# A 32-expert feed-forward sublayer: four slot tiles a step instead of two, products on column and row groups

## What is computed

```python
E = 32
H = int(D * 0.25)          # D = 128
logits = x_flat @ router_w.T + router_b
routed_idx = jnp.argmax(logits, axis=-1)
def expert_mlp(w1, b1, w2, b2):
    h = jax.nn.relu(x_flat @ w1 + b1)
    return jax.nn.relu(h @ w2 + b2)
y_all = jax.vmap(expert_mlp)(weights1, bias1, weights2, bias2)
out_flat = y_all[routed_idx, jnp.arange(n)]
...
x = _layernorm(x + _L1_ffn_ref(x, ...), axis=-1)
```

## Time and profile before

| what | value |
|---|---|
| time, median of 3 runs | 4104.81 us (4103.65 to 4107.08) |
| time of the profiled execution | 4081.88 us |
| its span | 4080.1 us |
| last load before its routing, first load of the next sublayer | 1759.8 and 2154.9 us |
| its first and last `evict` | 1859.0 and 2087.6 us |

### The profile page before, as it was taken

The page is one execution under the profiler, slowest core; times in us unless marked ns, Lnnn a source line. Parts: engine busy times, 40 slices in busy tenths (PEclk is TensorE's granted clock), DMA queues, the critical chain, the costliest instruction groups (busy, mean ns, idle before and its releaser), DMA issues. The chain is left out here.

```text
span 4080.1 us, 81328 instructions
## 1 busy us (share of the span) xinstructions
PE 3018.0 (74%) x27802; PEld 2047.6 (50%) x27802; DVE 2256.7 (55%) x6213; ACT 1718.3 (42%) x3334; POOL 1789.2 (44%) x1575
## 2 busy tenths in 40 slices
PE   3399907767777599946747996886899867997693
PEld 2387805554455356634524664554344434666572
DVE  2002336536777577751235775886777576775123
ACT  0144404334444366602214664664555554662341
POOL 2544272225565455523344554664022354552534
PEclk9999959888998799955558998998898788997896
DMA  6377611020010112114521112221000001221573
GB/s 215 115 227 218 191 41 45 6 7 24 32 41 31 53 55 73 55 41 122 136 76 41 55 53 67 76 86 59 1 1 1 1 3 47 77 67 56 160 224 106
DMA packets 305037, 304.44 MB, mean 75 GB/s; under 512 B 91108, under 2 KB 226821, under 8 KB 304648
## 3 DMA queue, kind: packets, MB, share of 16 engines
q1 hardware_dynamic: 269160, 252.01, 20.1%
q0 software_dynamic: 16384, 33.59, 2.8%
q10 hardware_dynamic: 19232, 15.50, 1.2%
HBM read 161.27 MB, written 55.84 MB: 53 GB/s over the span
## 5 line engine op out<-in xcount | busy, mean ns | idle before, releaser
L802 DVE TENSOR_TENSOR moe_first_tile_y<-moe_first_out_ps,moe_first_expert_w 128x256 f32<-128x256 f32 x78 | 33.1, 425 | 336.5 <-PE moe_first_out_ps L937 336.4
L998 POOL DMA_INDIRECT slot_x<-x_tok,moe_first_slots x128 | 123.7, 967 | 177.8 <-DVE moe_first_slots L775 75.1
L978 ACT ACTIVATE moe_first_hid<-moe_first_hid_ps,moe_first_expert_w 128x256 f32<-128x256 f32 x312 | 128.2, 471 | 155.6 <-PE moe_first_hid_ps L926 155.6
L1012 POOL DMA_INDIRECT moe_first_token_y<-slot_y,moe_first_slots x128 | 123.8, 967 | 100.4 <-issue 65.2
L1665 POOL TENSOR_TENSOR causal_k_blocks<-causal_k_T,headmask 128x1024 f32<-128x1024 f32 x64 | 121.2, 1896 | 105.9 <-PE causal_scores L1277 101.9
L2783 PE MATMUL L_ffn_experts<-L_ffn_expert_w,x_T 128*128 128x512 f32 x256 | 166.2, 735 | 1.8 <-ACT L_ffn_expert_out L2880 1.8
L1665 POOL TENSOR_TENSOR alibi_k_blocks<-alibi_k_T,headmask 128x1024 f32<-128x1024 f32 x64 | 121.2, 1896 | 105.2 <-PE alibi_scores L1277 101.2
L1665 POOL TENSOR_TENSOR full_k_blocks<-full_k_T,headmask 128x1024 f32<-128x1024 f32 x64 | 121.2, 1896 | 93.8 <-PE full_scores L1277 89.5
L937 PE MATMUL moe_first_out_ps<-moe_first_expert_w,moe_first_hid 128*128 128x128 f32 x1248 | 162.2, 281 | 0.0
L1416 ACT ACTIVATE diff_probs_T<-diff_pT 128x512 f32<-128x512 f32 x128 | 76.4, 597 | 183.0 <-PE diff_pT L1291 183.0
L1665 POOL TENSOR_TENSOR keys_k_blocks<-keys_k_T,headmask 128x1024 f32<-128x1024 f32 x64 | 120.7, 1896 | 74.7 <-PE keys_scores L1277 71.1
(11 more groups left out here) (544 smaller groups left out, 9152.3 us busy)
## 6 DMA issues: line engine op xcount, KB each, us to landing
moe_first_expert_w<-in_L_attn_experts SPq DMA_DIRECT2D x78, 578.0 KB, 4.0
moe_last_expert_w<-in_L_ffn_experts SPq DMA_DIRECT2D x46, 578.0 KB, 4.1
slot_x<-blank ACTq DMA_DIRECT2D x2, 4992.0 KB, 44.2
moe_first_tile_x<-slot_x SPq DMA_DIRECT2D x78, 128.0 KB, 4.1
slot_y<-moe_first_tile_y SPq DMA_DIRECT2D x78, 128.0 KB, 1.9
L_ffn_tile_x<-slot_x SPq DMA_DIRECT2D x64, 128.0 KB, 2.3
slot_y<-L_ffn_tile_y SPq DMA_DIRECT2D x64, 128.0 KB, 1.8
moe_last_tile_x<-slot_x SPq DMA_DIRECT2D x46, 128.0 KB, 3.9
```

Of the source, the lines that this page charges most:

```text
L802: dve.tensor_tensor(y_out[:, q, :, :], out_bank[q][:, 0:SLOT_TILE].rearrange("p (s d) -> p s d", s=SPAN), over(wall[:, j % RING, 2 * FF + ...
L978: act.activation(hid[:, j % 2, b, :], hid_bank[b // 2][:, SLOT_TILE * (b % 2):SLOT_TILE * (b % 2) + SLOT_TILE], gelu, bias=wall[:, j % RIN ...
L998: pool.indirect_dma_start(slot_x[part][:, :], bass.IndirectOffsetOnAxis(slots[:, part, r, t:t + 1], 0), net.x_tok[:, part * K + t, :], Non ...
L1012: pool.indirect_dma_start(y_in[:, p, k, r, :], None, slot_y[part][0:NT * SLOT_TILE, :], bass.IndirectOffsetOnAxis(slots[:, part, r, t:t + ...
```

## The change

Four slot tiles, a "quad" (`QUAD` = 512 rows), are one step; there are 16 steps a part, 32 in all. The four first products write to the four partition groups of one bank, [32g, 32g + 32), so that each has a 32-column group of the array; one relu of 128x128 covers all four. The second products read the hidden rows at partitions [32g, 32g + 32), so that each has a 32-row group, and each writes a bank of its own. Their bias is no longer a 33rd row but a product of its own, of 32 rows of ones with the bias row of the expert's block (its other 31 rows are zero). An expert's weights come in two transfers, `up` (128 rows of 128 B) and `down` (32 rows of 1028 B), where one of 128 rows of 644 B was. The output has one set of four banks that does not alternate. `x_in` has three places of a quad.

```diff
-    J = NT // 2
+    J = NT // 4
-    RING, XRING = 8, 4
+    RING, XRING = 4, 3
...
-        x_in = sb("tile_x", [128, XRING, 2, D])
-        hid = sb("hid", [H + 1, 2, PAIR])
+        x_in = sb("tile_x", [128, XRING, 4, D])
+        hid = sb("hid", [128, 2, TILE])
...
+        out_banks = ctx.enter_context(nc.psum_tensor(f"{name}_out_ps", [128, 4, 512], F32))
...
-        after_pair = {J + 2 + c * ((J - 4) // PC): c for c in range(PC)}
+        after_quad = {J + 2 + (5 * c + 2) // 3: c for c in range(PC)}
...
# evict
-                    dve.tensor_copy(y_out[:, q, :, :], out_bank[q][:, 0:PAIR].rearrange("p (s d) -> p s d", s=2))\
-                        .then_inc(out_done, 1)
+                    dve.tensor_copy(y_out[:, q, :, :], out_banks[:, :, 0:D]).then_inc(out_done, 1)
...
+            def load_expert(eng, j, g):
+                part, n = divmod(j, J)
+                at = 4 * n + g
+                if j >= RING:
+                    eng.wait_ge(out_ready, j - RING + 1)
+                if n == 0:
+                    eng.wait_ge(planned, 2 * part + 2)
+                e = eng.value_load(expert_of[0:1, part, at:at + 1], min_val=0, max_val=E - 1)
+                eng.dma_start(up[:, j % RING, g, :], w_up[bass.ds(e, 1), :, :].rearrange("o p h -> p (o h)"))\
+                    .then_inc(w_landed[j % RING], 16)
+                eng.dma_start(down[H * g:H * g + H, j % RING, :], w_down[bass.ds(e, 1), :, :].rearrange("o p w -> p (o w)"))\
+                    .then_inc(w_landed[j % RING], 16)
...
# SyncE's queue
                 for j in range(ALL):
+                    if j + 2 < ALL:
+                        load_slots(j + 2)
                     if j + 3 < ALL:
-                        load_expert(sp, 2 * (j + 3))
+                        load_expert(sp, j + 3, 0)
+                    store_slots(j)
                     if j + 3 < ALL:
-                        load_slots(j + 3)
-                    store_slots(j)
-                    if j - 2 in after_pair:
-                        tail.store(sp, after_pair[j - 2])
+                        load_expert(sp, j + 3, 2)
...
# turn
-                    for s in range(2):
+                    for s in range(4):
...
# hidden
+                    for g in range(4):
+                        last = pe.matmul(hid_bank[j % 2][H * g:H * g + H, 0:TILE], up[:, j % RING, g, :],
+                                         xT[:, j % 2, TILE * g:TILE * g + TILE], start=True, stop=True)
...
# output
-                    if j >= 2:
-                        pe.wait_ge(out_done, j - 1)
+                    if j >= 1:
+                        pe.wait_ge(out_done, j)
+                    for g in range(4):
+                        lane = slice(H * g, H * g + H)
+                        pe.matmul(out_banks[:, g, 0:D], net.ones[lane, :], down[lane, j % RING, D + 1:W], start=True, stop=False)
+                    pe.wait_ge(hid_done, j + 1)
+                    for g in range(4):
+                        lane = slice(H * g, H * g + H)
+                        last = pe.matmul(out_banks[:, g, 0:D], hid[lane, j % 2, :], down[lane, j % RING, 0:D],
+                                         start=False, stop=True)
...
-                    if j - 2 in after_pair:
-                        tail.transpose(pe, after_pair[j - 2], xT_bank)
+                    if j - 1 in after_quad:
+                        tail.transpose(pe, after_quad[j - 1], xT_bank)
```

More of the change, by code:

```diff
@@ L2358, in _ @@
                     evict(j)
-                    if j in after_pair:
-                        combine(after_pair[j])
-                    if j - 1 in after_pair:
-                        tail.normalise(dve, after_pair[j - 1])
+                    if j in after_quad:
+                        combine(after_quad[j])
+                    if j - 1 in after_quad:
+                        tail.normalise(dve, after_quad[j - 1])
                 for c in late:
@@ L2433, in count @@
                         for h in range(2):
-                            last = pe.matmul(banks[h][:, :], w[:, :], flat[:, HALF * h:HALF * h + HALF], start=True, stop=True)
+                            last = pe.matmul(banks[h], w[:, :], flat[:, HALF * h:HALF * h + HALF], start=True, stop=True)
                     last.then_inc(ranked, 1)
@@ L2498, in relu @@
                     act.wait_ge(hid_ready, j + 1)
-                    for s in range(2):
-                        t = 2 * j + s
-                        act.activation(hid[0:H, j % 2, TILE * s:TILE * s + TILE],
-                                       hid_bank[j % 2][0:H, TILE * s:TILE * s + TILE], ACT.Relu,
-                                       bias=wall[0:H, t % RING, H:H + 1]).then_inc(hid_done, 1)
+                    act.activation(hid[:, j % 2, :], hid_bank[j % 2][:, 0:TILE], ACT.Relu,
+                                   bias=down[:, j % RING, D:D + 1]).then_inc(hid_done, 1)
                 for j in range(3):
-                    load_expert(act, 2 * j + 1)
+                    for g in (1, 3):
+                        load_expert(act, j, g)
                 for j in range(-2, ALL):
@@ L2512, in _ @@
                     if 0 <= j and j + 3 < ALL:
-                        load_expert(act, 2 * (j + 3) + 1)
-                    if j - 2 in after_pair:
-                        tail.copy_transposed(act, after_pair[j - 2], xT_bank)
+                        for g in (1, 3):
+                            load_expert(act, j + 3, g)
+                    if j - 1 in after_quad:
+                        tail.copy_transposed(act, after_quad[j - 1], xT_bank)
                 for c in late:
@@ L3067, in run @@
             if n == 6:
-                moe_small(net, final, "L1_ffn", w["L1_ffn_experts"])
+                moe_small(net, final, "L1_ffn", w["L1_ffn_up"], w["L1_ffn_down"])
             if n == 7:
@@ L3135 @@
     up, up_b, down, down_b = (np.asarray(inputs[f"L1_ffn_{k}"]) for k in ("weights1", "bias1", "weights2", "bias2"))
-    packed = np.zeros((32, 128, 32 + 1 + D), np.float32)
-    packed[:, :, 0:32] = up
-    packed[:, 0:32, 32] = up_b
-    packed[:, 0:32, 33:] = down
-    packed[:, 32, 33:] = down_b
-    arrays["L1_ffn_experts"] = packed
+    arrays["L1_ffn_up"] = np.ascontiguousarray(up)
+    packed = np.zeros((32, 32, D + 1 + D), np.float32)
+    packed[:, :, 0:D] = down
+    packed[:, :, D] = up_b
+    packed[:, 0, D + 1:] = down_b
+    arrays["L1_ffn_down"] = packed
     for k in ("weights1", "bias1", "weights2", "bias2"):
```

67 lines of the change are left out of this document (26 added, 41 removed).

## The result

The changed kernel takes 4157.66 us (4153.54 to 4163.42), the kernel before 4105.92 us beside it: a ratio of 1.0125, 95% interval 1.0109 to 1.0141, or **52 us more**. Forecast were 4146 and +41.

A forecast was written before the change was run, and what follows sets the result against it. No full engine but a ring of waits (eviction, store issue, rows load, TensorE) was taken to set the pace. A turn of 2.8 + 3.0 + 3.25 = 9.05 us against 7.26 gave +41 us: 4146 us, range 4115 to 4185.

The forecast's parts named there:

- The step that decided the sign: On TensorE `turn(j + 3)` directly follows `output(j)`, so one turn passes one quad and 2.7 us are no longer covered.
- eviction and SPq: From the eviction's start on VectorE through SPq's store and weight issues to the rows load: 2.8 us, bounds 2.6 to 3.4.
- the load: Transfer of a quad's rows from DRAM, 256 KB: 3.0 us against 2.42 for 128 KB, bounds 2.4 to 3.6.
- transposes: Four transposes on TensorE from `turn` to the start of `hidden`: 1.05 us.
- `hidden`: First products on TensorE, eight passes on four column groups: 0.65 us, 0.56 if groups work at once, 1.84 if not.
- `output`: Second products on TensorE, sixteen passes with the bias product: 1.5 us, 1.22 if four groups work at once, 3.8 if serial.
- Start and end: Around the loop: first eviction 2.0 us later, last two quads 2.3 us each, last store landing 0.6 us later.
- The term that was put at nothing and was not: Scatter of part 1 and the gathers, on GpSimd: costed at nothing, having 16 steps of more time than before.
- Groups one after another: Packing fails on TensorE and groups run serially: turn 12.5 us, in all about 4250 us; chance 0.08.
- Small rows slow: Small weight rows hold the load at 3.6 us or more: turn 9.7 to 10.3, 4165 to 4182 us; chance 0.14.
- The clock: TensorE's clock rises to 2.4 GHz: turn 7.4 us, in all 4095 us, faster than before; chance 0.05.
- Near no change: All terms of the turn at their low ends: turn 7.9 us, +5 to +8 us; chance 0.05.

The follow-up runs named there:

- run 1: Changed kernel with each quad's rows load one step earlier (three quads loaded ahead instead of two): 3987.87 us, ratio 0.9798 to the kernel before.
- run 3: Kernel before, its pairs and own products kept, with two pairs loaded ahead instead of three: 4274.0 us, ratio 1.050.
- run 5: Changed kernel, no edit, measured again on another chip: 4109.04 us, ratio 1.0092 to the kernel before.
- runs 5 and 10: Changed kernel, no edit, measured again on two chips: 4109.04 us, ratio 1.0092, and 4161.81 us, ratio 1.0121.
- run 11: Changed kernel with even quads evicted by four single-bank copies, odd ones by one copy over four banks: 4111.38 us, ratio 1.0113.
- runs 8 to 10: One chip: changed kernel with output products tile by tile, 1.0119; rows behind store, five quads ahead, with fixed experts, 0.9809; changed kernel unedited, 1.0121.

## Why the prediction held, and where it was off

**The step that decided the sign** was that `turn(j + 3)` directly behind `output(j)` leaves nothing under the load, so that one turn passes one quad. Shown three times: by the 29 waits for the rows, by run 1, which gives the cover back and lands at 0.98, and by run 3, which takes it from the pairs and costs 210 us. That the packing is not to blame is shown by run 1, which keeps all of it, and by run 3, which has none.

**The terms.** Of the forecast 9.05 us, eviction and SPq were 2.8 (2.74 in most turns and 2.78 in the mean, with a hole of 0.11 us between the two weight issues where 0.1 was taken), the load 3.0 (in the mean of the first part 3.15 in the first profile and 3.07 in run 5), transposes 1.05 (1.05), `hidden` 0.65 (0.58), `output` 1.5 (1.24, near the packed end of 1.22) and the hand-over 0.05 (0.07). The turn is 8.78 to 8.86 us, so the sum was 0.2 to 0.3 too long, nearly all of it `output`: 16 passes were hardly held by their weight loads. The load's 0.1 us more takes a part of that back. The prediction weighed the Trainium skill, "TensorE: Matmul & The Clock Gate", where four row groups of 32 give 3.07 times and not 4. The estimate from it, 0.60 for `hidden` and 1.23 for `output`, is within 0.02 us of the trace, and its turn of 8.7 was nearer than mine. But this does not tell 3.07 from 4: the prediction's own value for four groups fully at once was 1.22, and `hidden` lies on column groups, for which that figure is not.

**Start and end.** The first eviction comes 9.3 us behind the first rows load (1879.51 us), 1.4 later than before, where 2.0 was forecast. The last two quads took 4.71 and 2.53 us and not 2.3 each: with no load left to cover them, one chunk's `normalise` (1.10 us) and four transposes (1.11) stand between the last eviction but two and the next `hidden`, and so on the path. The part after the loop took 66.5 us for 67.3. Twenty-nine turns of 8.78 us (run 5) in place of 9.05 are 8 us less, and the last two quads give back 2.6. So the loop is 33 us longer where 38.5 was forecast, and the whole kernel in run 5 is 35 us slower by its medians, 37 by the ratio: without late evictions the forecast was some 5 us too high.

**The term that was put at nothing and was not** is the one on GpSimd: "The scatter of part 1 and the gathers have 16 steps of more time than now". They have, and the part after the loop is unchanged, as forecast. But in the first result TensorE's signals are late behind the gathers, and that puts 14 us into the loop. So +41 came close to +52 partly by luck: 5 us too much in the terms stand against 14 that were not foreseen, and 2 are not accounted for. The kernel before has nothing of the kind in its profile, but that profile is itself of the other kind: 4081.88 us in all where the runs beside it gave 4104.81, and no part of VectorE's wait in the first sublayer put down to "remote". What its 64 evictions lose where the signals are late was not seen in a trace. That the ratio there is 1.012 and not 1.009 is only a hint that the quads lose more (the intervals of runs 5 and 10 overlap, and run 11, with no late eviction, has 1.0113); the likely reason, not tested, is that each late eviction goes straight into a ring that has no slack.

**The rivals.** Groups one after another: no; the first passes of `hidden` on the four groups start within 0.02 us. Small rows slow: no, the load took 3.07 to 3.15 us in the mean. The clock: 0.50 throughout. Near no change: its low ends held for `hidden` and `output` alone (0.58 and 1.24 for 0.56 and 1.22).

What stays open is why TensorE's signals are late behind GpSimd's indirect transfers, and why only in some profiles: those of the first result and of runs 8 to 10 show it, those of all other runs, on three chips, and that of the kernel before don't. On which chip that last one was taken is not known, so for the first result's chip it is not shown that the lateness is always there.

## What to carry to other kernels

Before packing or widening a step, count how many steps one turn of the ring of waits passes, and count it again after: a step that got twice as large, with fewer of them in flight, can give all its gain back. If one step lies under the load today, the new order must keep one there; here that was a difference of one in a loop index, worth 3%. When the order was right here, the next bound was the queue that issues transfers: register reads between issues fill it although the profile doesn't count them as busy. And when an engine starts late, look up the signal that it waits for: here the engine that looked slow was waiting for another's. And when a change is costed against one profile, see whether that profile's own time is that of the runs it will be compared with.

## What the hardware showed that was not expected

- Products on four row groups do not need neighbours in program order. Tile by tile or pass by pass, sixteen passes and the hand-over took 1.36 and 1.31 us; the first passes of all four tiles still start within 0.05 us, ahead of tile 0's product on the hidden rows, which the code has in front of the other tiles' bias.
- The same kernel on different chips took 4064 to 4115 us. In the first result and on the chip of runs 8 to 10, TensorE's signals to VectorE and ScalarE come up to 14 us late (up to 6.5 us in the loop) behind rows of GpSimd's indirect gathers and scatters, in touched and untouched sublayers, while TensorE itself works on and the other engines' signals are on time. On three other chips no signal is over 0.3 us late.
- A rows load issued 0.43 us behind a store of 256 KB was waited for 0.3 us longer than one issued 2.02 us behind it, at a DMA share of 0.45. The cause was not tested.
